# A state-space and mixture-of-experts layer on one core: Silu blocks of one expert instead of two, and another order in the first sequence

## What is computed

```python
# selective layer: 256 inner channels x 64 states per sequence
delta = softplus(d_raw @ Wdt + bdt)
dA = exp(delta[..., None] * A)          # decays
h  = dA * h + (delta * x) * B           # a scan over 512 tokens
y  = C * sum(h, -1)                     # states summed

# mixture: two of eight experts count for each token
logits = xf @ Wg
top_w, top_i = top_k(logits, 2); top_w = softmax(top_w)
combine = einsum('nk,nke->ne', top_w, one_hot(top_i))
y = einsum('enh,ehc->enc', silu(xf @ W1[e]) * (xf @ W2[e]), W3[e])
out = einsum('enc,ne->nc', y, combine)
```

## Time and profile before

| | |
|---|---|
| median of 3 runs | 1852.05 us (1850.15 to 1855.08) |
| the profiled execution's own time | 1861.63 us |
| its span, first to last instruction | 1859.7 us |
| instructions | 19053 |
| granted TensorE clock, mean | 0.860 |

### The profile page before, as it was taken

The page is one execution under the profiler, slowest core; times in us unless marked ns, Lnnn a source line. Parts: engine busy times, 40 slices in busy tenths (PEclk is TensorE's granted clock), DMA queues, the critical chain, the costliest instruction groups (busy, mean ns, idle before and its releaser), DMA issues.

```text
span 1859.7 us, 19053 instructions
## 1 busy us (share of the span) xinstructions
PE 1351.0 (73%) x5928; PEld 617.7 (33%) x5928; DVE 1514.5 (81%) x2105; ACT 1281.5 (69%) x2275; POOL 1513.9 (81%) x888
## 2 busy tenths in 40 slices
PE   4336458777886887778776878778787778668958
PEld 1001123234342343324342343324332343324535
DVE  4879988898889889898899888888888988895222
ACT  4547668687877778777777778777787777755423
POOL 0899999978998799977998899987998799983312
PEclk9557569889987989879897989879898898979979
DMA  3601411122111311132101401132111321100000
GB/s 87 212 34 71 164 46 51 49 91 97 57 40 48 148 51 33 54 104 96 55 25 50 162 29 51 49 106 81 51 51 49 102 85 52 46 29 1 7 1 6
DMA packets 38747, 121.89 MB, mean 66 GB/s; under 512 B 5875, under 2 KB 21110, under 8 KB 26358
## 3 DMA queue, kind: packets, MB, share of 16 engines
q1 hardware_dynamic: 37062, 120.67, 18.3%
q10 hardware_dynamic: 1584, 0.01, 0.0%
HBM read 109.13 MB, written 11.53 MB: 65 GB/s over the span
## 4 chain that ended last, share of the span: by engine, by line
PE 27%; ACT 18%; DVE 15%; POOL 14%; issue 8%; DVEq 0%; POOLq 0%; ACTq 0%
DVE h L1251 10%; POOL w L947 9%; PE bankH L565 8%; ACT da L837 5%; PE bankY L579 5%; PE bankG L565 5%; ACT yk L798 4%; ACT L837 3%; PE ys L633 2%; POOL x L890 2%; PE bankG L512 2%; DVE aq L1189 1%; PE bankY L559 1%; ACT L785 1%; ACT sq L785 1%
## 5 line engine op out<-in xcount | busy, mean ns | idle before, releaser
L1251 DVE TENSOR_TENSOR_SCAN h<-da,w 128x512 f32<-128x512 f32 x1024 | 1192.1, 1206 | 158.3 <-ACT da L837 133.0
L947 POOL TENSOR_TENSOR w<-ur,br 128x1024 f32<-128x1024 f32 x512 | 1193.6, 2365 | 33.1 <-DVE h L1251 21.2
L837 ACT ACTIVATE da<-dr,al 128x511 f32<-128x511 f32 x1024 | 681.9, 687 | 221.9 <-DVE h L1251 212.5
L633 PE MATMUL ys<-h,wsum 128*32 128x512 f32 x2048 | 320.9, 703 | 208.5 <-DVE h L1251 189.2
L565 PE MATMUL bankH<-nT,w 128*128 128x512 f32 x512 | 301.8, 673 | 89.7 <-DVE aq L1189 85.3
L890 POOL TENSOR_TENSOR x<-x,yk 128x512 f32<-128x512 f32 x128 | 163.1, 1274 | 211.2 <-ACT yk L798 210.6
L579 PEld LDWEIGHTS bankY<-w,aq 128*128 128x128 f32 x2048 | 262.8, 203 | 87.0 <-issue 65.0
L579 PE MATMUL bankY<-w,aq 128*128 128x128 f32 x2048 | 270.5, 289 | 12.4 <-DVE aq L1189 7.9
L565 PE MATMUL bankG<-nT,w 128*128 128x512 f32 x432 | 243.8, 648 | 24.6 <-DVE aq L1189 24.6
L798 ACT ACTIVATE yk<-bankY,rt 128x128 f32<-128x128 f32 x512 | 151.8, 364 | 121.5 <-PE bankY L579 107.8
L633 PEld LDWEIGHTS ys<-h,wsum 128*32 128x32 f32 x2048 | 42.9, 115 | 408.5 <-DVE h L1251 373.2
(11 more groups left out here) (187 smaller groups left out, 1135.8 us busy)
## 6 DMA issues: line engine op xcount, KB each, us to landing
br<-b_rows SPq DMA_DIRECT2D x64, 1024.0 KB, 5.0
dr<-d_rows SPq DMA_DIRECT2D x16, 1024.0 KB, 7.1
ur<-u_rows SPq DMA_DIRECT2D x16, 1024.0 KB, 8.4
d_rows<-vh SPq DMA_DIRECT2D x16, 256.0 KB
u_rows<-th SPq DMA_DIRECT2D x16, 256.0 KB
xnew<-in_L_attn_a_x_dram SPq DMA_DIRECT2D x8, 256.0 KB, 5.3
...
```

The costliest lines, as they stand in the source:

```text
L633: ins = nc.tensor.matmul(ys[32 * q:32 * q + 32, :], wsum[:, :], h[:, (DUOS * t.b + 2 * group + q // 2) % H_RING, q % 2, :], start=(n == 0) ...
L837: A(da[duo % D_RING][:, k % 2, 1:L], dr[:, half, q, 1:L], ACT.Exp, scale=nega[:, QUADS * half + q, n:n + 1]).then_inc(decay_ready, 1)
L947: G.tensor_tensor(w[:, turn_duo % W_RING, :, :], ur[:, half, q:q + 2, :], br[:, chunk % B_RING, row:row + 1, :].to_broadcast([128, 2, L]), ...
L1251: V.tensor_tensor_scan(h[:, turn_duo % H_RING, k % 2, :], da[duo % D_RING][:, k % 2, :], w[:, turn_duo % W_RING, k % 2, :], 0.0, ALU.mult, ...
```

## The change

**Blocks.** The four tiles of a quarter are no longer handled as one block. Each expert has a block of its own two tiles: tile 0 in bank H, tile 1 in bank G, both for `h` and for `g`. The second expert of a quarter stands 5 slots behind the first (`EXPERT_STEPS`), its successor 6 slots behind it. Bank Y holds no tile now. The outputs stand 7 and 13 slots behind the quarter's start instead of 9 and 13 or 14. In the late half the experts stand at slots 0, 5, 10 and 15.

**First sequence.** The constants of the diagonal layer move behind the two `vh` instructions; the matrices are copied out of PSUM ahead of the table of cosines, whose scratch is now in PSUM bank Y; POOL's product for sequence 0 waits for the tiles of `xs` alone and not for those of `sres`.

**Router and W3.** W3 stays as it is: `scale_outputs` is gone. ScalarE makes `0.5 * tanh + 0.5` in a second instruction (Identity), and VectorE makes `(R2 - R1) * that + R1`, one instruction less.

```diff
-GATED_STEPS, OUTPUT_STEPS = (2, 3, 7, 8), (9, 13)
+EXPERT_STEPS, OUTPUT_STEPS, GATED_STEPS = (0, 5), (7, 13), (2, 3)
-LATE_OUTPUTS = {3: 0, 4: 7, 5: 14, 6: 18, 7: 23}
-IN_THREE = ((1, 1), (1, 2), (1, 3), (2, 1), (2, 3))
-TWO_BANKS = ("HGHG", "HGHG")
-THREE_BANKS = ("HGYH", "GHGH")
-THREE_STEPS = (2, 4, 7, 8)
+LATE_EXPERTS = {4: 0, 5: 5, 6: 10, 7: 15}
+LATE_OUTPUTS = {3: 0, 4: 7, 5: 13, 6: 18, 7: 23}
 def silu_at(m, j):
-    return MOE_AT[m] + QUARTER_SLOTS * (j // 4)
+    return MOE_AT[m] + QUARTER_SLOTS * (j // 4) + EXPERT_STEPS[j // 2 % 2]
 def tile_slot(m, j, step=0):
-    at = silu_at(m, j) + step
-    return max(0, at - PAIRS) if is_late_tile(m, j) else at
+    return (LATE_EXPERTS[j // 2] if is_late_tile(m, j) else silu_at(m, j)) + step
+def bank_of(j):
+    return "HG"[j % 2]
...
-SETUP_AT = PRE_AT + 10
-MATRICES_AT = PRE_AT + 11
+SETUP_AT = PRE_AT + 17
+MATRICES_AT = PRE_AT + 17
-ROUTE = 14
+ROUTE = 13
...
-                        if n == 0:
-                            pe.wait_ge(outputs_scaled, QUADS)
...
-                        act.wait_ge(gap_ready, 2 * c + m)
-                        A(rc[:, 2, :], rc[:, 3, :], ACT.Tanh, scale=0.5).then_inc(gap_tanh_ready, 1)
+                        act.wait_ge(gap_ready, 3 * (2 * c + m) - 2)
+                        A(rc[:, 2, :], rc[:, 3, :], ACT.Tanh, scale=0.5).then_inc(gap_ready, 1)
+                        act.wait_ge(gap_ready, 3 * (2 * c + m) - 1)
+                        A(rc[:, 2, :], rc[:, 2, :], ACT.Identity, bias=half_col[:, 0:1], scale=0.5).then_inc(gap_ready, 1)
...
-            def scale_outputs():
-                for n in range(QUADS):
-                    yield SCALE_AT + 3 * n
-                    ...
-                    G.tensor_scalar(part, part, 0.5, None, ALU.mult).then_inc(outputs_scaled, 1)
...
-                        for m in range(4):
+                        for m in range(2 if known(i, 1) else 4):
                             pool.wait_ge(drained[BANK[f"in{m}"]], t.before(f"in{m}") + 1)
...
                 yield TURN_AT
+                v.wait_ge(matrices_turned, 1)
+                link(V.tensor_copy(mb[:, :, :].rearrange("p n c -> p (n c)"), banks["Y"][:, 0:256]))
+                link(V.tensor_copy(mc[:, :, :].rearrange("p n c -> p (n c)"), banks["Y"][:, 256:512]))
...
-                    one, two = rT[:, 0:n], tq[:, 0, 0:n]
+                    one, two = banks["Y"][:, 0:n], banks["Y"][:, 256:256 + n]
-                    link(V.tensor_tensor(S(19), s_, s_, ALU.mult))
-                    link(V.scalar_tensor_tensor(s_next, s_, 2.0, c_, ALU.mult, ALU.mult))
+                    link(V.tensor_scalar(S(19), s_, s_, None, ALU.mult))
+                    link(V.tensor_scalar(s_next, s_, c_, 2.0, ALU.mult, ALU.mult))
...
-                link(V.tensor_tensor(R(5), R(2), R(1), ALU.add))
-                v.wait_ge(gap_tanh_ready, 2 * c + m)
+                v.wait_ge(gap_ready, 3 * (2 * c + m))
-                drain(f"lg{m}", V.tensor_tensor(rt[:, 0, :, :], R(4), R(5), ALU.add))
+                drain(f"lg{m}", V.tensor_tensor(rt[:, 0, :, :], R(4), R(1), ALU.add))
```

More of the change, by code:

```diff
@@ L59, in tile_slot @@
 def tile_slot(m, j, step=0):
-    at = silu_at(m, j) + step
-    return max(0, at - PAIRS) if is_late_tile(m, j) else at
-def in_three(m, j):
-    return (m, j // 4) in IN_THREE
-def bank_of(m, j, gated):
-    return (THREE_BANKS if in_three(m, j) else TWO_BANKS)[gated][j % 4]
-def gated_step(m, j):
-    return (THREE_STEPS if in_three(m, j) else GATED_STEPS)[j % 4]
-def behind_third(m, e):
-    return e % 2 == 1 and in_three(m, 2 * e + 2)
+    return (LATE_EXPERTS[j // 2] if is_late_tile(m, j) else silu_at(m, j)) + step
+def bank_of(j):
+    return "HG"[j % 2]
 def output_slot(m, e):
@@ L88, in output_slot @@
         return LATE_OUTPUTS[e]
-    return silu_at(m, 2 * e) + OUTPUT_STEPS[e % 2] + (1 if behind_third(m, e) else 0)
+    return MOE_AT[m] + QUARTER_SLOTS * (e // 2) + OUTPUT_STEPS[e % 2]
 def weigh_slot(m, e, n):
-    at = output_slot(m, e) + WEIGH_LAG
-    if behind_third(m, e):
-        return at + 1 + n
-    return at + 1 if e % 2 == 0 and in_three(m, 2 * e + 4) else at + n
+    return output_slot(m, e) + WEIGH_LAG + n
 S5_AT = output_slot(1, E - 1) + SUM_LAG - 3
@@ L126 @@
         _kind = "late" if is_late_tile(_m, _j) else "post"
-        PE_STEPS.append((tile_slot(_m, _j), _kind, bank_of(_m, _j, False), f"h{_m}_{_j}"))
-        PE_STEPS.append((tile_slot(_m, _j, gated_step(_m, _j)), _kind, bank_of(_m, _j, True), f"g{_m}_{_j}"))
+        PE_STEPS.append((tile_slot(_m, _j), _kind, bank_of(_j), f"h{_m}_{_j}"))
+        PE_STEPS.append((tile_slot(_m, _j, GATED_STEPS[_j % 2]), _kind, bank_of(_j), f"g{_m}_{_j}"))
     for _e in range(E):
@@ L297, in hybrid_kernel @@
         scaled_ready = sem("scaled_ready"); x1_ready = sem("x1_ready"); shifted_ready = sem("shifted_ready")
-        gap_ready = sem("gap_ready"); gap_tanh_ready = sem("gap_tanh_ready"); routed = sem("routed")
+        gap_ready = sem("gap_ready"); routed = sem("routed")
         weighted = sem("weighted"); added = sem("added")
@@ L948, in pair @@
                                     br[:, chunk % B_RING, row:row + 1, :].to_broadcast([128, 2, L]), ALU.mult).then_inc(product_ready, 1)
-                weave(pair, [gates(t)] + ([scale_outputs()] if known(t.b, 1) else []) + tasks_of(t, pre_a, post, late))
+                weave(pair, [gates(t)] + tasks_of(t, pre_a, post, late))
             turns(pre_a, scan, post, late)
@@ L982, in _ @@
             chain(V.memset(one_col[:, :], 1.0))
+            chain(V.memset(half_col[:, :], 0.5))
             chain(V.memset(mhalf[:, :], -0.5))
@@ L1081, in diagonal_setup @@
                     link(V.scalar_tensor_tensor(sinT[:, n:2 * n], sinT[:, 0:n], c_, two, ALU.mult, ALU.add))
-                    link(V.scalar_tensor_tensor(c_next, c_, c_, S(19), ALU.mult, ALU.subtract))
+                    link(V.tensor_scalar(c_next, c_, c_, S(19), ALU.mult, ALU.subtract))
                     settle()
@@ L1086, in diagonal_setup @@
                 link(V.tensor_scalar(rT[:, :], cosT[:, :], 0.0, er, ALU.mult, ALU.add))
-                v.wait_ge(matrices_turned, 1)
-                link(V.tensor_copy(mb[:, :, :].rearrange("p n c -> p (n c)"), banks["Y"][:, 0:256]))
-                link(V.tensor_copy(mc[:, :, :].rearrange("p n c -> p (n c)"), banks["Y"][:, 256:512]))
                 settle()
@@ L1149, in R @@
                 def R(n):
-                    if n in (1, 3, 5):
+                    if n in (1, 3):
                         return rt[:, n, :, :]
```

9 lines of the change are left out of this document (3 added, 6 removed).

## The result

The changed kernel takes 1859.76 us (median of 6 runs, 1858.89 to 1862.69), the kernel before 1851.2 us (6 runs, 1847.98 to 1855.08): ratio 1.0046, 95% interval 1.0034 to 1.0058. It is slower by 0.46%. The forecast was 1813 us.

What follows compares the result with a forecast made beforehand. No engine is full; waits between engines bound the kernel, chiefly VectorE's stall behind ScalarE blocks, with POOL just under. Blocks 27 plus first sequence 12 make 39 us off the profiled 1861.63: 1822.6, or 1813 by median; whole range 1782 to 1866.

Steps and rivals of the forecast that it cites:

- The bound: Whole turns: VectorE's stall behind a ScalarE block, 16.5 us waiting for decays, is the largest removable item, POOL just under.
- The blocks, 4 us gained a turn: Expert blocks of two Silus: 4 us gained a turn, 27 us in all; bounds 9 us gained, 4 us lost.
- All tiles are now filled before their block starts.: Expert blocks: reason ScalarE's 7.4 us of waits before Silus shrink, 3.4 of it before third and fourth tiles.
- a `yk` waits for an output matmul that stands behind eight tiles, now behind four or five: TensorE's order in the expert pieces: reason the waits for `yk` shrink (ScalarE 9.1 us, POOL 14.2 us a turn).
- The loads: ScalarE: 108 more table loads at 1.28 us add 138 us, 20.5 a whole turn, and still fit its idle time.
- The tail, 0 within 2: Tail after the turns: TensorE's same work in two banks instead of three leaves 164.80 us unchanged, within 2 either way.
- First sequence, 12 us: Setup and turn 0: 6 us from earlier starts plus 6.1 from dropping POOL's four scalings; bounds 6 to 14.
- step (c): Setup: cosine table starts about 1.2 us later and waits 1.5 for transposes; VectorE free at 50 to 51.5.
- Router, 0: Routings: one more small ScalarE Identity, one less VectorE addition; 5 us if uncovered, taken as 0.
- both cancel: Rival for the whole kernel: blocks lose 1 to 2.5 us a turn, 1846 to 1858 us; chance 0.08.
- ScalarE takes over: Slower rival: each block drains the decay ring and five slots don't refill it; 5.5 us a turn, 1877; chance 0.24.
- POOL takes over: Rival: stalls go but POOL's work and other waits end each turn; 0 to 2 us gained, 1827 to 1842; chance 0.18.

Runs made afterwards that it cites:

- e8_z4_ln: e3_z4 with the first layer norm of post moved two slots later (9 instead of 7); 1846.37 us, ratio 0.9959 to the kernel before.
- e3_z4: Changed kernel with the matmuls of `z` at slot 4 instead of 5, ahead of the late tiles; 1845.78 us, ratio 0.9965 to the kernel before.
- e4_z4_tanh: e3_z4 with Tanh in place of Silu in the experts, so no table loads beside the blocks; 1810.33 us, ratio 0.9777 to the kernel before.
- e5_start_tanh: e1_start with Tanh in place of Silu in the experts, blocks of four; 1817.65 us, ratio 0.9807 to the kernel before.
- e2_blocks: Kernel before with the blocks of two Silus alone; start, W3 and router as before; 1869.95 us, ratio 1.0098.
- e1_start: Kernel before with all edits but the blocks (first sequence, unscaled W3, router), blocks of four Silus kept; 1839.12 us, ratio 0.9937.
- e7_order_only: Kernel before with only the first-sequence reordering and PSUM scratch, W3 still scaled and router as before; 1850.01 us, ratio 0.9975.

## Why the prediction was wrong

**The bound.** "... the largest removable item is the stall of DVE behind an ACT block" is the reading that failed. The 16.5 us of the earlier trace rows were taken as removable. e8_z4_ln removed 2.7 us of such a stall in turn 4, and 19 us of such waits over the kernel (93.4 instead of e3_z4's 112.6), and got nothing; e4_z4_tanh cut the waits for decays of turn 4 to 6.2 us and its turn was within 1 us of that of e5_start_tanh, which has 9.2. From slot 10 or so to slot 28 such waits fall in time that VectorE has to spare, for POOL works through; that the same holds in the other pieces is likely by these two runs, not shown row by row.

**The blocks, 4 us gained a turn.** This is the term that failed. It measured 3.4 us lost in turn 4 (215.06 against 211.71), just inside the bound of 4 lost, and e2_blocks, tail included, lost 18 us where the sum had 27 gained. The sign named for this case is there: a turn over 214 with the waits before `yk` and the Silus longer than before. Three steps under it:

- *"All tiles are now filled before their block starts."* Only for `sq` in bank H: 0.1 us of wait. `tq` in H rose from 1.9 to 3.2, `tq` in G from 2.1 to 2.7, `sq` in G is 2.6, where `sq` in G and Y had 1.4. With two banks each `h` tile waits for the `aq` that empties the same bank, and each block has a second tile that comes late. 7.9 us became 8.6, where the forecast had them shrink.
- *"... a `yk` waits for an output matmul that stands behind eight tiles, now behind four or five."* The order on TensorE, shown with the change, has seven tile matmuls ahead of the first output where eight stood, so the count was misread. And it left out who else shares TensorE's queue at the slot. At slot 5 two `h` tiles came ahead of `z`, and `z` ahead of the next output; POOL's wait for `yk` rose from 14.2 to 18.5. The order shown to the reader was that of the second mixture's first quarter, not of the seam, where the late experts moved from one block to four slots and crossed `z`. This one collision is 15 us of the kernel (e3_z4), some three quarters of what the blocks cost.
- *The loads.* 138 us of loads were counted rightly as work (66.71 us of ScalarE in slots 28 to 72 against 66.7 forecast) but priced at nothing beyond the fit into the idle time. By e4_z4_tanh and e5_start_tanh the mean turn pays 5.6 us for its loads with short blocks and 3.2 with long ones, turn 4 pays 4.3 and 3.4: 2.4 or 0.9 us a turn more.

Together, by mean turns: short blocks bring 0.8 us without loads, their loads take 2.4, and the late `z` takes 1.8 (215.0 less 213.2), 3.4 us net (215.0 less 211.6). By turn 4 alone, which is a usual turn in each kernel, the same 3.4 us are 0.1 brought, 0.9 for the loads and 2.65 for the late `z` (215.06 less 212.41). The net loss is firm, its split is not, because e3_z4's mean has two turns made longer by the clock; the medians, 14.0 us between the changed kernel and e3_z4 of 20.6 between it and e1_start, lean to the second split. The profiles of these two are 27.7 us apart: 4.0 ahead of the first scan, five turns of 3.3, 1.5 and 0.3 us in turns 1 and 7, and 5.4 in the tail. The medians lie 20.6 apart, the one profiled execution being 2.9 us over its median and the other 4.3 under.

**The tail, 0 within 2.** It is 4.5 us longer in the changed kernel, 2.7 in e2_blocks and 2.4 in e3_z4, TensorE's busy time in it 137.50 us instead of 132.61. That two banks leave TensorE less room than three where it is the bound is the likely reason, but no run tried the tail alone. The changed kernel's 2 us over e3_z4 are not the blocks: 1.7 of them arise between the tail's fifth and sixth sum on POOL, where TensorE's granted clock over 8 us was 0.57 (from 1726.64) and e3_z4's 0.79 (from 1708.77), as e2_blocks' was (from 1734.45), with the same order of work.

**First sequence, 12 us.** Right in sum, 11.7 us by the start of turn 1 and 11.7 by e1_start's ratio. `w` came at 46.33 and the scaling is worth 6.8 instead of 6.1. The first scan, forecast near 50.5, came at 53.92, 25.0 us behind the copy of `bcs` (26.7 before). The 49.95 of e1_start looks like a hit but is luck: that execution was 5.1 us earlier at the copy, and its scan is 26.2 us behind it. The two waits of step (c) were sized well (1.29 us for the logarithm, 1.52 for the transposes). What it missed are lengths: two small additions of the constants took 0.94 and 1.23 us instead of 0.15, beside POOL's product at 31.64, and the table took 12.77 us against 13.17, although two of its instructions had lost 1.1 us each beside POOL's product in before, so its small instructions did not keep their length. It cost nothing in the end, since POOL, which began on time, has 155.03 of turn 0's 156.46 us.

**Router, 0.** No run took it alone. e1_start contains it, and its turns are 211.6 us, as those of e7_order_only without it, so 0 fits.

**The rivals.** By time, *both cancel* (1846 to 1858) ends 1.8 us below the measured 1859.76, and *ScalarE takes over* at 4 us a turn has 1867; by the loss of 3.4 a turn the second is the nearer. It was said to decide from 16.7 us of ScalarE's waits above the ring in the three pieces. They are 161.1 less 141.1, 20.0 us in all, of which the ring is at most 3.7, so it stood about at the threshold. But its mechanism, that every block drains the ring, is not what is seen: the scans' waits for decays shrank. *POOL takes over*, at 0 to 2 us gained a turn, names what e4, e5 and e8 show of the blocks in themselves. The Trainium skill (ScalarE: Activation LUTs, "Rules for kernel authors") wants all work of one table set done before switching; the 5.6 us a turn that e4_z4_tanh saved speak for it. The drain of 1.38 us beside each load that the same page gives is again not in the trace: from the load at 851.20 to the Silu at 852.49 it is 1.29 us.
